# A graph network on one core: the gate stage's scans laid out by channel, its carries placed by a one-hot product, its table cleared in an earlier stage

## The reference, cut to what matters

```
x_flat: 8192 nodes x 128;  edge_index: 2 x 524288, values up to 32767 (a destination outside the
                           8192 nodes is dropped, a source outside is clipped to the last node)
h     = (x_flat @ W_gat).reshape(M, HEADS=4, NUM_EXPERTS=4)
a_src = (h * att_src).sum(-1);   a_dst = (h * att_dst).sum(-1)
e     = leaky_relu(a_src[src] + a_dst[dst], 0.2)          # edges and self loops
e_max = segment_max(e, dst);     ee = exp(e - e_max[dst]) # softmax over the edges of one node
denom = segment_sum(ee, dst);    agg = segment_sum(h[src] * ee / denom[dst], dst) + b_gat
scores = layernorm(agg).reshape(M, 4, 4).mean(1)          # then top 2 of 4, softmax -> gates
```

## Time and profile before

| | |
|---|---|
| median of 3 runs | 6109.43 us (6106.77 to 6116.88) |
| the profiled execution's own time | 6126.31 us |
| its span, first to last instruction | 6124.6 us |
| TensorE busy with products | 3980.3 us, 65% of the span |
| VectorE, ScalarE, GpSimd busy | 3161.4, 1620.0, 889.4 us |
| TensorE's mean granted clock | 0.862 of full speed |
| bytes moved by DMA | 497.29 MB |

### The profile page before, as it was taken

One profiled execution on the slowest core, in us unless ns is written; L12 is line 12 of the kernel. 1 busy time (PEld: TensorE's weight loads), 2 busy tenths in 40 slices (PEclk: granted clock), 3 DMA queues, 4 the chain that ended last, 5 costly groups with the idle time before them and its releaser, 6 DMA issues. The chain is left out here.

```text
span 6124.6 us, 70264 instructions
## 1 busy us (share of the span) xinstructions
PE 3980.3 (65%) x20835; PEld 2388.5 (39%) x20835; DVE 3161.4 (52%) x6562; ACT 1620.0 (26%) x2620; POOL 889.4 (15%) x923
## 2 busy tenths in 40 slices
PE   0003495588888888882200005993999958999999
PEld 0002384344444444441200003662555536666666
DVE  8999986566666666667233103126121263444443
ACT  0000042166666666662000001221000002222222
POOL 0000120277600000000477370000000000000000
PEclk9999987799999999996555557995999977999999
DMA  1000001165655555551111810000333320000000
GB/s 55 0 0 0 0 0 70 56 223 209 219 203 221 203 221 204 222 206 41 16 21 21 316 13 10 0 1 14 98 99 99 99 58 2 4 5 3 5 3 5
DMA packets 212486, 497.29 MB, mean 81 GB/s; under 512 B 66003, under 2 KB 93707, under 8 KB 211468
## 3 DMA queue, kind: packets, MB, share of 16 engines
q1 hardware_dynamic: 154716, 417.18, 19.7%
q10 hardware_dynamic: 29808, 71.57, 3.0%
q0 software_dynamic: 27840, 7.35, 1.3%
HBM read 361.26 MB, written 134.74 MB: 81 GB/s over the span
## 5 line engine op out<-in xcount | busy, mean ns | idle before, releaser
L1414 PE MATMUL at_out<-at_pt,g_H 128*128 128x512 f32 x2048 | 1201.1, 671 | 215.6 <-DVE at_pt L1351 215.6
L1266 ACT ACTIVATE at_rl<-at_qrow,at_less,at_steep 128x512 f32<-128x512 f32 x1024 | 829.8, 813 | 515.6 <-DVE at_pt L1351 515.6
L1626 PE MATMUL at_out<-at_parts,at_a 128*128 128x387 bf16 x4096 | 679.4, 329 | 63.6 <-issue 63.6
L1351 DVE SCALAR_TENSOR_TENSOR at_pt<-at_rl,at_turned 128x512 f32<-128x512 f32 x1024 | 660.8, 684 | 5.3 <-DVE top_X L1338 3.1
L1345 DVE CAST at_turned<-at_tp 128x512 uint8<-128x512 f32 x512 | 353.8, 691 | 546.2 <-PE at_tp L1407 479.8
L1407 PEld LDWEIGHTS at_tp<-at_identS,at_adj 128*128 128x128 fp8e4 x4096 | 327.2, 102 | 631.1 <-issue 631.1
L1626 PEld LDWEIGHTS at_out<-at_parts,at_a 128*128 128x128 fp8e4 x4096 | 399.5, 98 | 343.1 <-issue 66.4
L1928 DVE TENSOR_TENSOR ex_HH<-ex_SL,ex_hp 128x512 f32<-128x512 f32 (+1 forms) x384 | 263.5, 686 | 405.1 <-ACT ex_SL L1920 405.1
L1414 PEld LDWEIGHTS at_out<-at_pt,g_H 128*128 128x128 f32 x2048 | 330.1, 202 | 314.5 <-DVE at_pt L1351 311.6
L1920 ACT ACTIVATE ex_SL<-ex_hp 128x512 f32<-128x512 f32 (+1 forms) x384 | 228.7, 596 | 750.6 <-PE ex_hp L1873 750.6
L1407 PE MATMUL at_tp<-at_identS,at_adj 128*128 128x128 bf16 x4096 | 406.8, 225 | 12.1 <-DVEq L1322 12.1
(11 more groups left out here) (504 smaller groups left out, 4616.5 us busy)
## 6 DMA issues: line engine op xcount, KB each, us to landing
at_adj<-in_adj_dram SPq DMA_DIRECT2D x512, 512.0 KB, 4.8
adjT<-at_turned ACTq DMA_DIRECT2D x128, 512.0 KB
at_a<-adjT SPq DMA_DIRECT2D x128, 512.0 KB, 3.6
runs<-runs_zeros SPq DMA_DIRECT2D x120, 384.0 KB, 3.5
plan<-sort_recs SPq DMA_DIRECT2D x1, 6168.0 KB, 16.0
runs_GT<-tab,runs_RC POOLq DMA_INDIRECT x352, 2.4
rec<-at_part POOLq DMA_INDIRECT x304
runs<-runs_RN ACTq DMA_DIRECT2D x22, 192.0 KB, 2.0
```

The costliest lines, as they stand in the source:

```text
L1266: nc.scalar.activation(RL[u % NBUF][:], qrow[:], ACT.Relu, bias=less[:], scale=steep[:, u:u + 1]).then_inc(relud, 1)
L1351: nc.vector.scalar_tensor_tensor(out=PT[u % NBUF][:], in0=RL[u % NBUF][:], scalar=1.0, in1=AT[u // JB % NAT][:, u % JB, :], op0=ALU.add, o ...
L1414: nc.tensor.matmul(OUT[:], H[:, u, :], PT[u % NBUF][:], start=(u == 0), stop=(u == T - 1)).then_inc(mult, 1)
L1626: ins = nc.tensor.matmul(OUT[:, g, x, 0:3 * D1], ones[c % NBUF][:, j, x * P:(x + 1) * P], parts[:, u].rearrange("p k d -> p (k d)"), start ...
```

## The change

It does the following.

1. **The clearing of `runs` moves.** The zeros are written over the whole table (131 transfers of 384 KB, the same form) by SyncE in the phase "count", from a tile that GpSimd sets to zero. The 120 transfers, their wait and the tile in "runs" go.
2. **The running state is laid out channel by channel.** Tiles are [P, channels, 17], with one column ahead of the 16 for the state carried in. The 28 scans of 16 elements become three: one of 4 x 17 = 68 elements for the held a_dst, one of 68 for the maxima, one of 20 x 17 = 340 for the sums. A column with factor 0 (or penalty -1e30) at the head of each channel starts it afresh. ScalarE makes three exponentials instead of one (64, 64 and 256 elements, the last written to all 16 channels), then copies the state back to row order (`RN`, 384 elements) ahead of the store.
3. **The carries are placed without a fetch.** VectorE makes two one-hot tiles from the first record of each partition and of the one after it (`first`, and a new small load `after`), multiplies the 40 carried values with one of them (`spread`, 40 x 64 elements), TensorE makes five products of 128 x 512 elements with the other, and ScalarE copies the 2,560 results to `CE`. The store of `carry`, the 64 fetches and `endq` go. GpSimd makes one row of counting numbers (128 elements) ahead of the 64 fetches of `runs`.
4. **The node phase reads `CE` with a stride**, since it is now [P, 40, 64].
5. The memsets at the head of "runs" are more and larger (`RW`, `same`, `pen`, `decay`, `own`, `sum_in`, some 1,360 elements), and stand ahead of VectorE's wait for the first record.

```diff
@@ sort_edges, phase "count"
+            clear = pc.sbuf("clear", [P, CHUNK, runs.shape[1]])
+                @block.gpsimd
+                def _(pool):
+                    nc.gpsimd.memset(clear[:], 0.0).then_inc(runs_clear, 1)
+                @block.sync
+                def _(sp):
+                    rows = runs.rearrange("(p t) c -> p t c", p=P)
+                    sp.wait_ge(runs_clear, 1)
+                    with sp.Fori(0, LMAX // CHUNK) as i:
+                        sp.dma_start(rows[:, bass.ds(i * CHUNK, CHUNK), :], clear[:]).then_inc(runs_out, 16)
+                    sp.wait_ge(runs_out, 16 * (LMAX // CHUNK))
-                    step(nc.vector.tensor_copy(endq[:], w[:, 6, :]))
@@ gate_nodes, phase "runs": SyncE
+                    sp.wait_ge(after_ok, 1)
+                    sp.dma_start(after[0:P - 1, :], rv[1:P, 0, :]).then_inc(after_in, 16)
-                    sp.wait_ge(fill_ok, 1)
-                    with sp.Fori(pairs, LMAX // (2 * CK)) as i:
-                        sp.dma_start(nv[:, bass.ds(i * (2 * CK), 2 * CK), :], zeros[:]).then_inc(fill_out, 16)
-                    sp.wait_ge(fill_out, filled)
@@ VectorE, one chunk
-                            for h in range(NH):
-                                a = step(nc.vector.tensor_tensor_scan(HOLD[b][:, 1:CK + 1, h], flag[:, 1, :], own[:, :, h],
-                                                                      HOLD[1 - b][:, CK, h:h + 1], ALU.mult, ALU.add))
+                            now(nc.vector.tensor_tensor_scan(flat(HOLD[b][:]), flat(same[:]), flat(own[:]),
+                                                             0.0, ALU.mult, ALU.add))
...
+                            dve.wait_ge(packed, k + 1)
+                            now(nc.vector.tensor_tensor_scan(flat(RW[b][:, 0:NH, :]), flat(pen[:]), flat(sum_in[:, 0:NH, :]),
+                                                             0.0, ALU.add, ALU.max))
...
-                            for c in range(S):
...
-                                ins = nc.vector.tensor_tensor_scan(RN[b][:, 1:CK + 1, NH + c], ex[:, 1, :, h], new,
-                                                                   RN[1 - b][:, CK, NH + c:NH + c + 1], ALU.mult, ALU.add)
+                            now(nc.vector.tensor_tensor_scan(flat(RW[b][:, NH:W, :]), flat(decay[:]), flat(sum_in[:, NH:W, :]),
+                                                             0.0, ALU.mult, ALU.add))
@@ ScalarE, one chunk
-                            nc.scalar.activation(ex[:], ex[:], ACT.Exp).then_inc(exp_ok, 1)
+                            nc.scalar.activation(sum_in[:, NH:2 * NH, 1:C1], ex[:, 0], ACT.Exp)
+                            nc.scalar.activation(decay[:, 0:NH, 1:C1], ex[:, 1], ACT.Exp)
+                            nc.scalar.activation(decay[:, NH:S, 1:C1].rearrange("p (h e) c -> p h e c", h=NH),
+                                                 ex[:, 1].unsqueeze(2).to_broadcast([P, NH, NE, CK]), ACT.Exp).then_inc(exp_ok, 1)
                             act.wait_ge(run_ok, k + 3)
-                            act.dma_start(nv[:, bass.ds(k * CK, CK), :], RN[b][:, 1:CK + 1, :]).then_inc(rn_out[b], 16)
+                            act.wait_ge(rn_out[b], i * 16 + 16)
+                            nc.scalar.copy(RN[b][:], RW[b][:, :, 1:C1].rearrange("p w c -> p c w")).then_inc(packed, 1)
+                            act.wait_ge(packed, k + 3)
+                            act.sem_inc(passed, 1)
+                            act.dma_start(nv[:, bass.ds(k * CK, CK), :], RN[b][:]).then_inc(rn_out[b], 16)
@@ phase "carry"
+                    nc.vector.tensor_tensor(spread[:], back[:].unsqueeze(2).to_broadcast([P, 2 * S, NF]),
+                                            off_hot[:].unsqueeze(1).to_broadcast([P, 2 * S, NF]), ALU.mult).then_inc(spread_ok, 1)
+                    nc.scalar.copy(CE[:], CP[:])
+                    CB = BANK // NF
+                    for c in range(0, 2 * S, CB):
+                        ins = nc.tensor.matmul(CP[:, c:c + CB, :], part_hot[:], spread[:, c:c + CB, :], start=True, stop=True)
-                    sp.dma_start(carry, back[:]).then_inc(carry_out, 16)
+                    nc.gpsimd.iota(count[:], pattern=[[1, P]], base=0, channel_multiplier=0,
+                                   allow_small_or_imprecise_dtypes=True).then_inc(counted, 1)
                     for f in range(NF):
                         pool.indirect_dma_start(RE[:, f, :], None, runs, bass.IndirectOffsetOnAxis(ap=endi[:, f:f + 1], axis=0)).then_inc(run_in, 16)
-                    pool.wait_ge(carry_out, 16)
-                    for f in range(NF):
-                        pool.indirect_dma_start(CE[:, f, :], None, carry, bass.IndirectOffsetOnAxis(ap=endq[:, f:f + 1], axis=0)).then_inc(carry_in, 16)
```

More of the change, by code:

```diff
@@ L809, in top_two, with gate_nodes @@
             src = left
-def gate_nodes(nc, ident, rec, tab, runs, carry, ctl, endi, endq, cont, repeat, b_gat, ln_gamma, ln_beta, gates):
+def gate_nodes(nc, ident, rec, tab, runs, ctl, endi, cont, repeat, b_gat, ln_gamma, ln_beta, gates):
     N, TW = tab.shape
@@ L833, in gate_nodes @@
         lastd = ph.sbuf("lastd", [P, 1])
+        first = ph.sbuf("first", [P, 2], I32)
+        after = ph.sbuf("after", [P, 2], I32)
         with Phase(nc, "runs") as pr:
@@ L926, in _ @@
-                            step(nc.vector.tensor_scalar(flag[:, 1, :], flag[:, 0, :], -1.0, 1.0, ALU.mult, ALU.add))
-                            step(nc.vector.tensor_scalar(flag[:, 2, :], flag[:, 0, :], -LOW, None, ALU.mult))
-                            dve.wait_ge(gt_in[b], i * (16 * CK) + 16 * CK + 16)
-                            now(nc.vector.tensor_tensor(own[:], GT[b][:, :, HE + NH:TW],
-                                                        flag[:, 0, :].unsqueeze(2).to_broadcast([P, CK, NH]), ALU.mult))
@@ L932, in _ @@
-                            for h in range(NH):
-                                a = step(nc.vector.tensor_tensor_scan(HOLD[b][:, 1:CK + 1, h], flag[:, 1, :], own[:, :, h],
-                                                                      HOLD[1 - b][:, CK, h:h + 1], ALU.mult, ALU.add))
-                            dve.wait_ge(dve_step, a)
-                            now(nc.vector.tensor_tensor(own[:], GT[b][:, :, HE:HE + NH], HOLD[b][:, 1:CK + 1, :], ALU.add))
-                            now(nc.vector.scalar_tensor_tensor(out=lg[:], in0=own[:], scalar=0.2, in1=own[:], op0=ALU.mult, op1=ALU.max))
@@ L945, in _ @@
-                            now(nc.vector.tensor_tensor(ex[:, 1, :, :], ex[:, 1, :, :], RN[b][:, 1:CK + 1, 0:NH], ALU.subtract))
+                            step(nc.vector.tensor_copy(DF[b][:, 0:1], DF[1 - b][:, CK:C1]))
+                            now(nc.vector.tensor_copy(DF[b][:, 1:C1], RC[b][:, :, 0]))
+                            dve.sem_inc(rc_read, 1)
+                            now(nc.vector.tensor_tensor(flag[:], DF[b][:, 1:C1], DF[b][:, 0:CK], ALU.not_equal))
+                            step(nc.vector.tensor_scalar(same[:, :, 1:C1], flag[:].unsqueeze(1).to_broadcast([P, NH, CK]), -1.0, 1.0, ALU.mult, ALU.add))
@@ L1001, in _ @@
                     nc.vector.memset(pen[:, 0:1], -LOW).then_inc(ends_ok, 1)
+                    step(nc.vector.tensor_scalar(node[:, 0:1], first[:, 0:1], LOGF, None, ALU.arith_shift_right))
+                    step(nc.vector.tensor_scalar(node[:, 1:2], first[:, 0:1], NF - 1, None, ALU.bitwise_and))
+                    step(nc.vector.tensor_copy(nodef[:], node[:]))
+                    step(nc.vector.tensor_tensor(final[:], first[:, 0:1], after[:, 0:1], ALU.not_equal))
+                    dve.wait_ge(counted, 1)
+                    step(nc.vector.tensor_scalar(part_hot[:], count[:], nodef[:, 0:1], final[:], ALU.is_equal, ALU.mult))
+                    step(nc.vector.tensor_scalar(off_hot[:], count[:, 0:NF], nodef[:, 1:2], None, ALU.is_equal))
                     dve.wait_ge(turned_ok, 1)
@@ L1098, in _ @@
                     step(nc.vector.tensor_scalar(free[:], cont[:], LOW, -LOW, ALU.mult, ALU.add))
-                    step(nc.vector.tensor_tensor(cm[:], CE[:, :, 0:NH], free[:].unsqueeze(2).to_broadcast([P, NF, NH]), ALU.add))
+                    step(nc.vector.tensor_tensor(cm[:], CE[:, 0:NH, :].rearrange("p c f -> p f c"), free[:].unsqueeze(2).to_broadcast([P, NF, NH]), ALU.add))
                     step(nc.vector.tensor_tensor(mm[:], RE[:, :, 0:NH], cm[:], ALU.max))
@@ L2023, in graph_network @@
             project_edges(nc, ident, x, X, L0_ffn_W_gat, L0_ffn_att_src, L0_ffn_att_dst, XT, tab)
-            gate_nodes(nc, ident, rec, tab, runs, carry, ctl, endi, endq, cont, repeat, L0_ffn_b_gat, L0_ffn_ln_gamma,
+            gate_nodes(nc, ident, rec, tab, runs, ctl, endi, cont, repeat, L0_ffn_b_gat, L0_ffn_ln_gamma,
                        L0_ffn_ln_beta, gates0)
```

143 lines of the change are left out of this document (76 added, 67 removed).

## The result

| | kernel before, beside it | kernel after |
|---|---|---|
| median of 4 runs | 6108.14 us (6106.77 to 6116.88) | 5969.33 us (5946.86 to 5978.71) |
| profiled execution, span | 6126.31, 6124.6 us | 5946.86, 5945.2 us |

The ratio is 0.9763 [0.9744, 0.9782], so the kernel is faster; the medians lie 139 us apart. The forecast was 5955 us in a range of 5942 to 5980. The two profiled executions differ by 179.4 us, and that is more than the change did, as the phases show.

A forecast was written before the change was run, and what follows sets the result against it. GpSimd's fetch issue was taken to bound the loop of "runs", with the clearing laid bare after it. Terms -75.9 - 79.4 + 0.5 + 0.3 = -154.5 us took the median from 6109.4 to 5955 us, range 5942 to 5980.

The forecast's parts named there:

- The bound: Loop of "runs": GpSimd's fetch issue, 1.26 us apart, sets the pace; VectorE's work is hidden but for the last chunk.
- The cover: Loop of "runs": VectorE's 7.25 us a chunk has 17.6 us of cover, so changing the scans there gains 0.
- issues of GpSimd above 1 us: One of the signs listed beforehand that would show the prediction wrong; no phase was named for it.
- The last chunk: End of the loop of "runs": new scans, exponentials and copy back shorten the exposed chain by 1.8 us, to about 5.4.
- The clearing: End of "runs": without the clearing the carry phase starts 75.9 us earlier, last chunk and head included; "count" pays +0.3.
- The barrier: Between "runs" and the carry phase: taken as 2 us, from nearest rows of 1.65 and 6.1 us.
- The first rival: Phase "count": the clearing's full DMA slows VectorE's or TensorE's loop, 68 us come back, 6023 us; chance 5%.
- The third rival: Phase "count": the clearing is not hidden and the kernel is slower, 6143 us at 3.5 us a transfer; chance 2%.
- the fourth: End of "runs": something else, say the last store, holds it, so only the fetches go; 6030 us; chance 2%.
- The carries: Carry phase: 64 fetches leave GpSimd's queue, a counting row comes, the rest is hidden beside the remaining fetches; -79.4 us.
- The second rival: GpSimd's issue slows beside new VectorE instructions, one fetch in four of 352 held; 75 us back, 6030 us; chance 4%.
- Node: Node phase: three instructions reading `CE` with a stride cost +0.5 us, between 0 and +1.1.

The follow-up runs named there:

- E3: Kernel before with only the loop of "runs" laid out by channel, three long scans a chunk; 6107.49 us, ratio 0.9992.
- E6: Changed kernel with ten more scans of 340 elements in each chunk, written to an unused tile; first to last fetch 498.4 us for 442.5.
- E1: Kernel before with only the clearing moved into the phase "count"; 6040.19 us, ratio 0.9875.
- E5: Changed kernel with the table cleared three times, 393 transfers instead of 131; count took 394.1 us for 270.9.
- E4: Changed kernel with VectorE's product in the carry phase made five times instead of once; 6124.16 us, the 64 fetches 86.9 us for 80.5.
- F1: Changed kernel with the carry phase's product reading PSUM instead of a copy in SBUF; 6212.35 us, the 64 fetches 78.8 us for 80.5.
- A1: The changed kernel again without an edit; 5960.58 us, ratio 0.9743 to the kernel before.
- E2: Kernel before with only the carries placed by the one-hot product, in node's new layout; 6024.78 us, ratio 0.9853.
- E8: The kernel before again, unedited, on a third chip; 6388.67 us.

## Why the prediction was right, point by point

**The bound.** GpSimd's issue sets the loop: E3 takes a third of VectorE's work in the loop away and gains nothing measurable. Right, and the rows that said so were the waits and the spacing of the fetches, not the busy shares.

**The cover.** "17.6 us of cover and needs 7.25 [...] lengthening it costs nothing up to 17.6." This step was wrong. E6 lengthened it by 9 us, to about 15, stayed under 17.6, and lost 56 us. A chunk's work isn't only hidden beside the fetches, it can also slow them. The sum did not suffer, because the changed kernel pays little: a loop 0.4 us longer, a longest issue of 1.30 us. That was luck: the prediction did not ask where the long scan would fall, and it falls just behind the start of an issue in 19 chunks of 21. Of my own signs of being wrong, one did come, "issues of GpSimd above 1 us", and it pointed at this step.

**The last chunk.** The term was -1.8 us and measured -1.2. The product with transposed reads took 0.78 us, where the -1.8 assumed no extra cost (0.43 for the same 256 elements before), and the copy back 0.83 us for 0.52. The scan itself, 0.87 for 0.92, was right.

**The clearing.** The term was -75.9 us with the head's +0.6; with the head it is -76.7, in E1 alone -76.0. The barrier took 0.8 us where I had chosen 2, which pays for the longer chain. In "count" nothing was lost: 0.98 us a transfer, 591 us for its end, phase -0.2 us. The first rival (count disturbed) is refuted: each turn of the loop beside full DMA kept its pitch of 1.74 us, though its VectorE instructions show some 0.73 us, at most 0.77, for 0.69. The third rival (not hidden) is refuted as it stands, and E5 shows its mechanism at work at three times the load. So is the fourth: nothing else held the end of "runs", which is 11.7 us now.

**The carries.** -79.4 us, measured -79.7 + 1.7 = -78.0. What was missing is the one held fetch, a term that I had put at nothing. The second rival named this mechanism with 4%, but priced it at one fetch in four of the loop, +75 us; it is one fetch of 64 in carry and almost none in the loop. I had weighed it by the worst issue beside short scans of 16 elements, 0.04 us long in excess. Scans of 0.16 us could not show it, as the last section works out. The better row would have been of a long instruction with two SBUF inputs. Beside the earlier trace rows the kernel before has just that, begun 0.26 us ahead of the issue of 1.79 us:

```profile
740.37 1.22 DVE L789 TENSOR_TENSOR place_OP<-sort_iotaF,sort_partB 128x1024 bf16<-128x1024 bf16 x1
```

And in its carry phase one `RE` fetch, begun just inside a scan of 0.41 us, took 1.09 us:

```profile
3510.69 0.41 DVE L1017 TENSOR_TENSOR_SCAN carry_VC<-carry_ex 20x128 f32<-20x128 f32 x1
3510.77 1.09 POOL L1045 DMA_INDIRECT gat_RE<-runs,top_endi  x1 [0.30 <-issue]
```

"SBUF — State Buffer" of the Trainium skill, section "SBUF: two separate sides", gives the rule as an exclusive hold for the whole instruction by whichever of the two starts first. For VectorE's side E4, E6 and F1 agree, down to the exemption of a PSUM input. The other side hardly shows: scans that began 0.12 us or more behind the start of an issue took their usual 0.87 us. The same page of the Trainium skill, section "Who interferes with whom", takes it, as inferred, that a `tensor_tensor` doesn't hold up descriptor writing; here it holds up the issue of an indirect DMA, 2.63 us for 0.94, and the measurement decides.

**Node.** +0.5, measured +0.8.

**The sum and the median.** -154.5 against -153.7 us in the touched phases. The steps' own errors, -0.8 at the clearing, +1.7 at the held fetch and under 0.6 elsewhere, partly cancel. The 14 us between 5955 and 5969 are not a term: four other runs of the same kernel (A1) have a median of 5960.58, and all 17 runs of before one of 6115.95, from which the same sum gives 5961.5, beside 5963.2 for the 8 runs of the change. The term mis-sized is the scatter: I gave 10 us, and the runs of a kernel spread over 11 (A1) to 34 (E3). The longest stretch whose length varies is the dense attention, by TensorE's clock. So the forecast was right in its size by its steps and in its last digits by nothing.

## What to carry to other kernels

Read each phase that ends in a barrier by itself: a transfer with no engine busy beside it costs its full length, and beside a loop with idle DMA engines it costs nothing as long as it is shorter. Where GpSimd's issues set the pace, halving VectorE's instructions gains nothing. But look at how long those are that read two SBUF tiles: an issue that begins inside one, with more than 0.19 us to go, is held until it ends. Give the long ones an input in PSUM, which was shown here for one product, or see that they start just behind an issue. Compare an edit's phases between traces, and not two whole times, when a stage that nobody touched moves by 20 us.

## What the runs showed of the hardware

A fetch issue of GpSimd costs 0.94 us, and 1.49 beside back-to-back scans of 0.87 to 0.90 us, 2.55 to 2.64 beside products of 2.82 us. With a PSUM input in that product it is 0.94 to 1.00. The long issues are those that begin inside the scan or product, and they end 0.75 to 0.82 us after it; an issue begun 0.12 us or more ahead of it takes 0.94 to 0.99 us. From 0.94 and 0.75 it follows that an instruction with less than 0.19 us left costs an issue nothing (an estimate), and the short scans of the kernel before, 0.16 to 0.18 us each, are all of that kind.

TensorE's granted clock in the dense attention isn't a constant of the kernel. In the changed kernel it is at 1.2 GHz, not 2.4, for part of the first stretch below, and full in the second. In the first TensorE had stood idle 4.11 us, and its next two products took 2.08 us where two take 1.08 at the full clock:

```profile
1300.00:1320.00 20.00, 15.18 (x68) 7.69 (x67) 8.95 (x15) 11.10 (x17) 15.17 (x16) 0.83 0.41 135
1420.00:1440.00 20.00, 15.50 (x77) 7.37 (x75) 15.14 (x29) 12.44 (x19) 14.70 (x17) 1.00 0.66 242
```

```profile
1310.12 2.08 PE L1452 MATMUL at_out<-at_pt,g_H 128*128 128x512 f32 x2 [4.11 <-DVE at_pt L1389]
```

With two levels, a mean clock of 0.93 over 1581.9 us and of 0.95 over 1558.5 puts TensorE at the lower one for about 220 us in the kernel before and 155 in the changed one (an estimate), whose phase was 23.7 us shorter. In the traces of the two kernels and of E1, E2, E3 and A1 the mean is 0.93, 0.94 and four times 0.95, and the phase 1621.7, 1608.1 and 1598.0 to 1602.0 us. Why the clock falls at a place in one run and not in another is open.

On two chips some loops ran slower, and engines stood for "issue" inside them: "place" with what follows it took 544 to 552 us for some 475, the dense attention 1649 to 1744. Not all loops did: the count phase kept its 271 us, and all from the first experts on kept its 2384 to 2386 us, the loops of the second attention and of the experts included. The kernel before lost more than the changed one: in two groups, 6343.24 against E4's 6124.16 us, and 6388.67 and 6452.92 against F1's 6212.35, 176 to 241 us instead of 153. These are single runs. Between E8 and F1, the pair with traces, 15 us of the excess are the loop of "runs" and 28 its end (122.8 and 17.4 us from the last fetch to the first of the carry phase); the dense attention goes the other way, 1714.7 us for E8 and 1736.4 for F1. The loop with 876 VectorE instructions took 499.4 us, the changed one's, with some 374, took 485. That fewer instructions are the reason fits, but was only argued; what stalls these loops is open.
